# Seven half products with shared sums in a tuned attention kernel: which engine reads each product, and where the last convolution tap stands

## What is computed

```python
mixed = x @ w_qkv                      # 512 -> 2048 (q) + 2048 (k) + 4096 (v) columns
z = x @ w_z                            # 512 -> 4096
windows = stack([xp[:, k:k + T, :] for k in range(4)], axis=2)
mixed = silu(sum(windows * conv_w, axis=2))      # causal convolution, four taps
...
def step(state, inp):
    state = state * exp(g_t)
    kv_mem = einsum('bhd,bhde->bhe', k_t, state)
    delta = (v_t - kv_mem) * b_t
    state = state + einsum('bhd,bhe->bhde', k_t, delta)
    out_t = einsum('bhd,bhde->bhe', q_t, state)
```

## Time and profile before

| | before |
|---|---|
| time, median of 3 runs | 4295.72 us (4293.87 to 4295.82) |
| the profiled execution | 4292.53 us, span 4290.5 us |
| mean granted TensorE clock | 0.979 |
| TensorE busy | 4038.1 us (94%) |
| VectorE busy | 3436.5 us (80%) |
| ScalarE busy | 2504.0 us (58%) |
| GpSimd busy | 1008.7 us (24%) |

### The profile page before, as it was taken

One profiled execution on the slowest core, in us unless ns is written; L12 is line 12 of the kernel. 1 busy time (PEld: TensorE's weight loads), 2 busy tenths in 40 slices (PEclk: granted clock), 3 DMA queues, 4 the chain that ended last, 5 costly groups with the idle time before them and its releaser, 6 DMA issues. The chain is left out here.

```text
span 4290.5 us, 82720 instructions
## 1 busy us (share of the span) xinstructions
PE 4038.1 (94%) x29435; PEld 2303.8 (54%) x29435; DVE 3436.5 (80%) x8528; ACT 2504.0 (58%) x5895; POOL 1008.7 (24%) x1110
## 2 busy tenths in 40 slices
PE   6899999999999999999999999998799999999999
PEld 4455555555555555555555555555444444444444
DVE  4788888888888888888888888887455989998940
ACT  2466666666666666666666666666545656564633
POOL 2223333333333333433333433322200000000000
PEclk9999999999999999999999999999999999999999
DMA  3223343333343433343333333333502545454520
GB/s 127 81 70 76 76 97 75 82 80 77 77 97 71 116 78 83 77 91 76 83 77 84 77 87 79 82 76 87 117 1 83 163 150 168 153 174 151 183 64 10
DMA packets 290730, 402.97 MB, mean 94 GB/s; under 512 B 25774, under 2 KB 125362, under 8 KB 290258
## 3 DMA queue, kind: packets, MB, share of 16 engines
q1 hardware_dynamic: 253458, 330.57, 25.1%
q0 software_dynamic: 36864, 67.13, 11.5%
HBM read 288.56 MB, written 113.25 MB: 94 GB/s over the span
## 5 line engine op out<-in xcount | busy, mean ns | idle before, releaser
L669 PE MATMUL bank<-x_blocks,rows_b 128*128 128x512 f32 x1920 | 915.3, 606 | 8.9 <-DVE raw L1270 5.7
L1369 DVE SCALAR_TENSOR_TENSOR conv<-raw,conv_w,conv 128x1024 f32<-128x1024 f32 x384 | 516.5, 1345 | 18.5 <-ACT conv L995 9.4
L669 PEld LDWEIGHTS bank<-x_blocks,rows_b 128*128 128x128 f32 x1920 | 355.3, 197 | 320.0 <-issue 286.3
L823 PE MATMUL bank<-w_out_unit,oT 128*128 128x512 f32 x1008 | 489.3, 608 | 0.9 <-ACT out_stage L918 0.9
L1114 ACT ACTIVATE k_scaled<-o 128x128 f32<-128x128 f32 x512 | 154.0, 302 | 409.5 <-DVE o L1405 298.1
L669 PE MATMUL bank<-x_blocks,w_pair 128*128 128x512 f32 x768 | 366.8, 607 | 16.7 <-DVE common L1267 16.7
L1649 PE MATMUL bank<-xnT_f,w_gu 128*128 128x512 f32 x704 | 323.1, 602 | 1.2 <-ACT xnT_f L2148 0.9
L1668 PE MATMUL bank<-w_down,hidden 128*128 128x512 f32 x704 | 316.8, 593 | 1.7 <-DVE x_blocks L1727 1.7
L1658 PE MATMUL bank<-xnT_f,w_gu 128*128 128x512 f32 x704 | 316.8, 593 | 0.5 <-DVE hidden L1689 0.5
L2218 ACT ACTIVATE step_decay<-dt,rate 128x512 f32<-128x512 f32 x256 | 183.5, 720 | 219.5 <-DVE h L2327 217.3
L1456 POOL DMA_DIRECT2D x_after<-out_stage x256 | 222.0, 870 | 347.8 <-ACT out_stage L918 342.0
(11 more groups left out here) (266 smaller groups left out, 8613.8 us busy)
## 6 DMA issues: line engine op xcount, KB each, us to landing
x_after<-out_stage POOLq DMA_DIRECT2D x256, 256.0 KB, 4.6
rows_b<-bc_rows SPq DMA_DIRECT2D x256, 256.0 KB, 3.5
rows_c<-bc_rows SPq DMA_DIRECT2D x256, 256.0 KB, 3.7
w_pair<-in_w_qkv SPq DMA_DIRECT2D x128, 256.0 KB, 3.4
decay<-gc_rows SPq DMA_DIRECT2D x64, 512.0 KB, 4.7
z<-z_rows SPq DMA_DIRECT2D x64, 512.0 KB, 4.9
z_rows<-x_blocks SPq DMA_DIRECT2D x96, 256.0 KB, 3.8
w_pair<-in_w_z SPq DMA_DIRECT2D x64, 256.0 KB, 3.2
```

The lines of the kernel that those rows point to most:

```text
L669: made = e.matmul(bank[:, :], weight[:, j, :], part(0, m)[:, j, :], start=j == 0 and step < 3, stop=j == 1, skip_group_check=True)
L823: made = e.matmul(out_rows(N, t)[:, :], turned_to(N, t)[:, r, :], w_out[:, N % 2, r, :], start=r == 0, stop=r == REP - 1)
L1369: e.scalar_tensor_tensor(acc, raw[:, i, tap:tap + T], conv_w[:, tap, col:col + 1], acc, ALU.mult, ALU.add).then_inc(on["conv"], 1)
```

## The change

It orders the seven products anew, with other sums (Winograd's form). Step 0 is written to `PROJ`; ScalarE copies it from there to the other bank, `ZB`. Steps 1, 3 and 5 go to `PROJ`, steps 2, 4 and 6 to `ZB`; all but steps 0 and 3 accumulate onto what is in their bank. ScalarE copies out the results of steps 1 and 6 and the partial sums of steps 2 and 3 (into `partial`); VectorE makes the results of steps 4 and 5 by one addition each. So ScalarE makes five reads of a pair and VectorE two. GpSimd makes four sums of 256 columns in place of one of 512 and three of 256. The next weights are loaded after step 6, before after step 4. Three products are now in slots 1, 2, 4, 5, 7, two in slots 0, 3, 6. A product of step 1 or 2 now waits for ScalarE's copy of step 0. The convolution's last tap moves from before read "b" to behind `o`; section 0 of `base_inverse` in slot 2 moves from the slot's end to before the taps.

```diff
-ORDER = (1, 2, 5, 4, 3, 7, 6)
+ORDER = (1, 2, 6, 5, 7, 3, 4)
-ACT_STEPS, DVE_STEPS = (0, 3, 4), (1, 2, 5, 6)
+ACT_STEPS, DVE_STEPS = (0, 1, 2, 3, 6), (4, 5)
-PLACE = {(0, 0): 2, (1, 1): 5, (0, 1): 3, (1, 0): 4}
-SUMS_AT = {1: 0, 2: 1, 5: 2, 7: 3, 6: 4}
+PLACE = {(0, 0): 1, (1, 0): 2, (0, 1): 4, (1, 1): 3}
+X_SUMS = {5: 1, 7: 2, 6: 3, 4: 4}
+SUMS_AT = {5: 0, 6: 1, 7: 2, 3: 3}
+RESULT = {1: (0, 0), 4: (1, 1), 5: (0, 1), 6: (1, 0)}
-    return -(-UNIT_PRODUCTS * k // PER_UNIT)
+    return (UNIT_PRODUCTS * k + 2) // PER_UNIT
...
-            return (PROJ, ZB)[g % 2]
+            return (PROJ, ZB)[ORDER[pair_step(g)[1]] in (6, 7, 4)]
...
-                    if step == 4 and pair + 2 < PAIRS * UNITS:
+                    if step == PRODUCTS - 1 and pair + 2 < PAIRS * UNITS:
...
@@ product(g) of TensorE
-                if g >= 2:
-                    if pair_step(g - 2)[1] in ACT_STEPS:
-                        e.wait_ge(on["act_read"], act_count(g - 2))
-                    else:
-                        e.wait_ge(on["dve_read"], dve_count(g - 2))
+                if step in (1, 2):
+                    e.wait_ge(on["act_read"], act_count(PRODUCTS * pair))
+                elif step in (3, 4, 5):
+                    e.wait_ge(on["act_read"], act_count(g - 2))
+                elif step == 6:
+                    e.wait_ge(on["dve_read"], dve_count(g - 2))
+                elif pair > 0:
+                    e.wait_ge(on["dve_read"], dve_count(g - 2))
...
-                    made = e.matmul(bank[:, :], weight[:, j, :], part(0, m)[:, j, :], start=j == 0 and step < 3, stop=j == 1,
+                    made = e.matmul(bank[:, :], weight[:, j, :], part(0, m)[:, j, :], start=j == 0 and m in (1, 5), stop=j == 1,
...
@@ before the slots, TensorE
+            e.matmul(ZB[:, :], c["ident"][:, :], part(0, 2)[:, 0, :], start=True, stop=True)
...
@@ read_product(g) of ScalarE
-                    e.mul(common[:, pair % 2, :], product_bank(g)[:, :], -1.0).then_inc(on["act_read"], 1)
+                    e.copy(ZB[:, :], bank).then_inc(on["act_read"], 1)
+                elif step in (2, 3):
+                    if pair > 0:
+                        e.wait_ge(on["dve_read"], len(DVE_STEPS) * pair)
+                    e.copy(partial[:, step - 2, :], bank).then_inc(on["act_read"], 1)
...
@@ read_product(g) of VectorE
-                if step in (1, 2):
-                    e.tensor_tensor(total, bank, total, ALU.add).then_inc(on["dve_read"], 1)
-                else:
-                    wait_result_free(e, unit, q, step)
-                    e.tensor_tensor(result_place(q, step), bank, total, ALU.subtract).then_inc(on["dve_read"], 1)
+                wait_result_free(e, unit, q, step)
+                e.tensor_tensor(result_place(q, step), product_bank(g)[:, :], partial[:, 5 - step, :], ALU.add).then_inc(
+                    on["dve_read"], 1)
...
@@ the slots of VectorE
+                n = unit_at_only(slot, 10)
+                if n is not None:
+                    base_inverse(n, 0, 0)
+                convolve(slot, (2, 1))
...
+                convolve(slot, (0,))
                 read_at(slot, "c")
...
                     n = unit_at_only(slot, 10 + 4 * a)
-                    if n is not None:
+                    if n is not None and a == 1:
                         base_inverse(n, a, 0)
...
@@ weight_sums of GpSimd
-                    if pair + 1 < PAIRS * UNITS and step in (2, 6):
-                        weight_sums(pair + 1, (1, 2) if step == 2 else (5, 6))
+                    if pair + 1 < PAIRS * UNITS and step in (3, 5):
+                        weight_sums(pair + 1, (5, 6) if step == 3 else (7, 3))
```

More of the change, by code:

```diff
@@ L317, in result_place @@
                 return z_stage[Z_STAGE[step]]
-            return {3: raw_place(2 * q + 1, 0), 4: raw_place(2 * q, 1), 5: raw_place(2 * q, 0), 6: raw_place(2 * q + 1, 1)}[step]
+            i, half = RESULT[step]
+            return raw_place(2 * q + i, half)
         def wait_result_free(e, unit, q, step):
             if q == Z_PAIR:
-                used = {3: 32 * unit, 4: 16 * unit, 5: 16 * unit, 6: 32 * unit + 16}[step]
+                used = {1: 32 * unit, 4: 16 * unit, 5: 16 * unit, 6: 32 * unit + 16}[step]
                 if used > 0:
@@ L326, in wait_result_free @@
             else:
-                tile = 4 * unit + 2 * q + (1 if step in (3, 6) else 0)
+                tile = 4 * unit + 2 * q + RESULT[step][0]
                 if unit > 0:
@@ L407, in store_z @@
                     e.wait_ge(on["dve_read"], dve_count(g))
-                r, half = {3: (1, 0), 4: (0, 1), 5: (0, 0), 6: (1, 1)}[step]
+                r, half = RESULT[step]
                 e.dma_start(z_rows(unit, r)[:, half * BANK:(half + 1) * BANK], z_stage[Z_STAGE[step]]).then_inc(
@@ L463, in sync @@
                     pair, step = pair_step(g)
-                    if pair % PAIRS == Z_PAIR and step >= 3:
+                    if pair % PAIRS == Z_PAIR and step in RESULT:
                         store_z(g)
@@ L897, in read_product @@
                 e.wait_ge(on["product"], g + 1)
+                bank = product_bank(g)[:, :]
                 if step == 0:
-                    if pair >= 2:
-                        e.wait_ge(on["dve_read"], len(DVE_STEPS) * (pair - 1))
-                    e.mul(common[:, pair % 2, :], product_bank(g)[:, :], -1.0).then_inc(on["act_read"], 1)
+                    if pair > 0:
+                        e.wait_ge(on["act_read"], act_count(g - 1))
+                    e.copy(ZB[:, :], bank).then_inc(on["act_read"], 1)
+                elif step in (2, 3):
+                    if pair > 0:
+                        e.wait_ge(on["dve_read"], len(DVE_STEPS) * pair)
+                    e.copy(partial[:, step - 2, :], bank).then_inc(on["act_read"], 1)
                 else:
                     wait_result_free(e, unit, q, step)
-                    e.copy(result_place(q, step), product_bank(g)[:, :]).then_inc(on["act_read"], 1)
+                    e.copy(result_place(q, step), bank).then_inc(on["act_read"], 1)
             def read_at(slot, place):
@@ L1285, in gate_out, with convolve @@
                             on["oT_copy"], 1)
+            def convolve(slot, taps):
+                for i in range(4):
+                    n = unit_at_only(slot, 2 + 2 * i)
+                    if n is not None:
+                        p = 4 * n + i
+                        col = first_tile(n % HK)[i]
+                        acc = conv[:, p % 3, :]
+                        e.wait_ge(on["tap3"], p + 1)
+                        for tap in taps:
+                            if tap < PAD - 1:
+                                e.wait_ge(on["conv"], 3 * p + PAD - 1 - tap)
+                            e.scalar_tensor_tensor(acc, raw[:, i, tap:tap + T], conv_w[:, tap, col:col + 1], acc,
+                                                   ALU.mult, ALU.add).then_inc(on["conv"], 1)
             row_stats(0)
@@ L1356, in vector @@
                 gate_out(slot)
-                for i in range(4):
-                    n = unit_at_only(slot, 2 + 2 * i)
-                    if n is not None:
[L1361 to L1370, removed]
+                n = unit_at_only(slot, 10)
+                if n is not None:
+                    base_inverse(n, 0, 0)
+                convolve(slot, (2, 1))
                 for a in range(2):
```

77 lines of the change are left out of this document (37 added, 40 removed).

## The result

| | before | after |
|---|---|---|
| time, median | 4295.77 us | 4167.59 us (4165.81 to 4173.55) |
| ratio | | 0.9705, 95% interval 0.9688 to 0.9722 |
| profiled execution, span | 4290.5 us | 4166.1 us |
| mean granted TensorE clock | 0.979 | 0.991 |

The change makes the kernel 3.0% faster, 128 us; 4188 us and a range of 4115 to 4250 us were forecast.

A forecast was written before the change was run, and what follows sets the result against it. TensorE was taken as the bound, its waits for VectorE and half clock as the gain. Savings of 3.45 us x 30 = 103.5 plus 4 in start-up took 4292.5 to 4185; 3.2 more gave a 4188 us median, range 4115 to 4250.

The forecast's parts named there:

- The bound: TensorE, busy 95%, bounds the kernel; 4.05 us of waits and 1.7 us of half clock a unit can be won.
- Slot 5: TensorE's wait for `resid` falls from 2.14 to 0.42 us, 0.5 with product "c"; the slot takes slot 1's old shape.
- Slots 7 to 1: TensorE waits 1.8 us in all for `state`, `resid` and ScalarE's copy (0.3), against 1.88 to 3.03 before.
- Slot 2, section 0: `state` comes 1.6 us later behind `oT`, but a third product of 1.72 us covers it: costs nothing.
- The clock: No wait over 1.5 us remains, and such waits were not followed by half clock: 1.7 us a unit won.
- rival (b): Waits go as forecast, but the clock still falls once a unit in or ahead of slot 1: 4239 us, chance 0.22.
- The start-up: Waits for VectorE's reads there, one of 5.12 us, lose their cause: 4 us won, between 0 and 11.
- VectorE's load: Six fewer reads a unit at 0.69 us, 4.1 us of its 78; VectorE near 74 us a unit.
- The meeting of VectorE with GpSimd: VectorE loses 0.7 us where their work coincides; one more meeting a unit ahead of slot 1 adds 21 us.
- (a): TensorE never waits, since VectorE, with eased load, arrives earlier in slot 7: 4119 us, chance 0.13.
- (c): Slower: ScalarE's copy in slot 0 comes late and product "c" waits; 4333 us if 3 us late, chance 0.07.
- (d): VectorE's freed time becomes idle time ahead of slot 1 and slot 2 waits as much: 4296 us, chance 0.03.

The follow-up runs named there:

- a_table: The change with the old table of slots (how many products stand in each slot): 4279.52 us, ratio 0.9963 to the kernel before.
- t_both: The change with one step of section 3 moved from slot 4 to slot 3 and section 1 put ahead of `oT`: 4168.09 us, ratio 0.9699.
- a_section0: The change with section 0 of slot 2 back at the slot's end: 4165.95 us, ratio 0.9699.
- b_table: The kernel before with the new table of slots alone (three products in slots 1, 2, 4, 5, 7): 4263.85 us, ratio 0.9924.
- a_tap: The change with all three taps ahead of `state` again, section 0 left ahead of them in slot 2: 4238.46 us, ratio 0.9866.
- b_tap_table: The kernel before with the change's table, tap and section 0, but its old seven products and reads: 4268.48 us, ratio 0.9937.
- b_tap: The kernel before with the last tap behind `o` and section 0 of slot 2 ahead of the taps, nothing else: 4285.34 us, ratio 0.9974.
- a_copy2: The change with ScalarE's copy from bank to bank made twice, three times a unit: 4188.22 us, ratio 0.975.
- a_delay3: The change with three idle VectorE operations behind section 3 in slot 4, ahead of the `resid` of slot 5: 4322.76 us, ratio 1.0065.

## Why the prediction was right, point by point

**The bound.** Right. TensorE's waits for VectorE and the half clock were what could be won. Per unit of the steady stretch the waits went from 4.2 us ((53.3 + 31.9 + 1.0) us in 1900, or 20.6 units) to 1.5, where 2.3 were forecast. The wait of 2.62 us for `state` that I took from the timeline was an exception: it is the only one of 21 in this window, the others are near 1.46.

What one fall of the clock costs can be read in the kernel before, in the one unit of the window that goes without it:

```profile
1533.63 0.71 PE L772 MATMUL bank<-resid,invT 128*128 128x128 f32 x4 [2.14 <-DVE resid L1311]
1624.16 0.93 PE L772 MATMUL bank<-resid,invT 128*128 128x128 f32 x4 [2.14 <-DVE resid L1311]
```

These are 90.53 us apart, and the same matmuls of a usual unit 92.15 (1346.79 to 1438.94): 1.6 us, forecast 1.7. With 2.7 us of waits that makes 4.3 us a unit, and a unit became 3.9 us shorter. The 0.4 us between are not explained; the list leaves out short waits.

**Slot 5.** Right: 0.46 us are left of 2.14, forecast 0.42 and 0.1 for product "c", which does not wait. `a_table` gives the slot most of its wait back, 1.56 us. That the slot would behave as slot 1 held too: `t_both` shows ScalarE's chain right behind.

**Slots 7 to 1.** Right in kind, 0.8 us too long. `oT` started 4.72 us after the slot (1392.80), forecast 4.7; TensorE reached L780 at 1416.47, 23.7 us after it, as forecast. From `oT` to the end of `resid` it was 19.93 us, forecast 20.65: section 1 took 4.4 with its `oT` and not 4.8, `state` and `o` 0.66 for 0.8, two taps 3.28 for 3.4. So the 0.4 us for `state` (19.2 us against 18.8) vanished, and only the 1.03 us for `resid` are left, where I had 1.8 in all and 1.3 as the least. The 0.3 us for the copy in slot 0 are not there: product "c" begins 0.05 us behind the copy (1406.24 to 1406.29), and no wait is listed.

**Slot 2, section 0.** Nothing, as forecast; `a_section0` shows it.

**The clock.** Right in the result, weaker in its reason. No window at half clock is left in the steady stretch. But I took "waits of 1.5 us were not followed by it" as a limit for one wait, and the length of one wait does not decide. In `a_table` a wait of 1.31 us is followed by 0.50, one of 1.56 us is not. The windows after these two waits:

```profile
1358.50:1361.50 3.00, 3.00 (x6) 1.40 (x5) 2.52 (x18) 0.46 (x2) 0.00 (x0) 0.50 0.00 0
1424.50:1427.50 3.00, 2.88 (x74) 2.31 (x75) 2.53 (x5) 2.99 (x5) 2.86 (x4) 1.00 0.66 132
```

Nor does the same wait do the same each time. In `b_table` TensorE waits 2.09 us for `state` at 1277.85 and 2.08 us at 1460.61; the windows behind them:

```profile
1278.00:1281.00 3.00, 3.00 (x7) 1.79 (x8) 2.74 (x13) 2.43 (x11) 0.00 (x0) 0.56 0.00 0
1461.00:1464.00 3.00, 3.00 (x11) 1.68 (x10) 2.71 (x13) 2.98 (x11) 0.00 (x0) 1.00 0.03 12
```

And in the kernel before, the wait of 2.14 us in slot 5, after which the earlier trace rows has 0.53, comes again one unit later, at 1533.63, with the full clock behind it:

```profile
1534.00:1537.00 3.00, 2.88 (x75) 2.06 (x74) 2.53 (x5) 2.98 (x5) 2.92 (x6) 1.00 0.43 38
```

So three windows were too few to read a limit from. What else decides isn't settled by these runs. What can be said is that waits of 1.03 and 0.46 us (the change) and of 1.15 and 0.8 (`a_tap`) were never followed by the half clock in this stretch. `b_tap_table`, with no wait over 1.6 us and the half clock still there, shows that my reason did not secure the result. That the full clock came back was in part luck, and rival (b), in which the clock still falls, had better grounds than I gave it.

**The start-up.** The step that failed in size: 4 us forecast, at most 11, and 17.6 measured. `a_table` and the change have their first `state` at 182.1 and 182.4 us, `b_tap_table` at 187.0, `b_table` at 189.1, `b_tap` at 196.7, before 200.0. With the new products the table makes no difference there; without them it takes 10 to 11 us off. In the first 205 us TensorE's products waited 25.6 us for VectorE's reads before (9.3, 5.1, 3.5, 3.2, 2.4 and 2.2) and 7.8 us after. I had named this wait and put only 4 us on it. The one of 5.1 us can be followed: VectorE makes batch statistics ahead of that read (L1201, L1204, 47.53 to 52.82 us). The clock was also higher, 1.00 where it was 0.90 from 100 to 150 us.

**The sum.** 31 units instead of 30, 3.91 us each in the middle instead of 3.45 and less at either end: 111.0 us for 103.5; start-up 17.6 for 4; the end 4.2 us longer, where I had nothing. That is 124.4 for 107.5.

**VectorE's load.** It fell by more than the reads: 1516.81 us in 21.5 units, 70.4 us a unit, where 74 were forecast (ScalarE has 60, forecast 61). Some 2.2 us of the rest has a cause that I had only as a risk, and no wait of TensorE is listed in slot 2 behind it. Before, the subtraction of slot 1 stood beside GpSimd's weight sums; now there are none in slot 1. Before, then after:

```profile
1394.57 3.47 DVE L1349 TENSOR_TENSOR decay<-decay,col_beta 128x1024 f32<-128x1024 f32 x1
```

```profile
1418.69 1.21 DVE L1371 TENSOR_TENSOR decay<-decay,col_beta 128x1024 f32<-128x1024 f32 x1
```

The meeting of VectorE with GpSimd that I set against the change worked for it here.

The copy to PSUM took 585 ns, that to SBUF 592. The Trainium skill (ScalarE: Activation LUTs, "Step-by-step: what each stage is for") has PSUM as the faster. The means here differ by 1% that way, but the shortest of each is 570 ns to PSUM and 564 to SBUF, so this trace does not bear it out clearly.

**Rivals.** (a) is what `t_both` tried: it took away all waits for VectorE, and those for ScalarE left it at 88.0 us a unit, the change at 88.2. (c): `a_copy2` delays each copy by some 0.6 us and costs 21 us, so the copy is near the path but does not set the time. (d) did not happen. (b) is under the clock above.

## What to carry to other kernels

Parts of a change to a kernel whose engines wait for each other don't add up: table 32 us, tap with section 0 11 us and both 28 us in the old kernel; taken out of the new one, the table costs 112 us and the tap alone 71. An engine that is late is helped twice, by giving it less to do and by giving the waiting engine something to do ahead of the wait; the first without the second (`a_table`) left 16 us of the 128, the second without the first (`b_tap_table`) 28. Before a wait is worked away, it pays to look how soon the next engine's result comes behind it.

## What the runs showed of the hardware beyond what was expected

- VectorE operations with two SBUF inputs stretch beside GpSimd's: 1.21 to 3.47 us for 1024 columns, 0.42 to 1.3 us (median in `a_delay3`; shortest 0.424, longest 1.499) for 256 columns. The one of 3.47 us (before, to 1398.04) ended 1.1 us after GpSimd's two weight sums (to 1396.95), near the 1.2 us that it takes alone. That fits an operation that was held until they were done and not one that ran slowly; one case does not prove it.
- A half-clock stretch came after single waits between 1.31 and 2.62 us, and failed to come after others of 1.47 and 1.56 us, and of 2.08 (`b_table`) and 2.14 us (before). The length of the wait alone did not decide.
